# The first pass over the up-projections stores its transposed weight blocks in DRAM, the second pass loads them; late adapter terms, operand slots and the start are reordered

## What is computed

```python
# layer 0: weights quantised to a codebook of 8, plus a rank-64 adapter
lora_delta = lora_B @ lora_A * 0.5
normalized = (weight + lora_delta) / exp(scale_log)          # groups of 128
w_eff = codebook[searchsorted(...)] * scale + lora_delta
x = x + x @ w_eff.T
# layer 1: gated MLP, H = 1024, F = 2752, a rank-16 adapter chosen for each batch row
gate = x @ W_gate.T + 0.5 * (x @ A_gate[i].T) @ B_gate[i].T
up   = x @ W_up.T   + 0.5 * (x @ A_up[i].T) @ B_up[i].T
act  = silu(gate) * up
x = x + act @ W_down.T + 0.5 * (act @ A_down[i].T) @ B_down[i].T
```

## Time and profile before

| | us |
|---|---|
| median of 3 runs | 1616.69 (1616.1 to 1617.36) |
| profiled execution | 1616.32 |
| its span, first to last instruction | 1614.7 |
| PE busy | 1576.9 (98%) |
| DVE busy | 1275.1 (79%) |
| ACT busy | 564.9 (35%) |
| POOL busy | 529.0 (33%) |
| granted TensorE clock, mean | 0.995 |

### The profile page before, as it was taken

How to read it: one execution, slowest core, us unless ns; L and a number is a source line. 1 busy time by engine, 2 the same in 40 slices (tenths; PEclk the granted TensorE clock), 3 DMA queues, 4 the chain that set the end, 5 groups by cost and what they waited for, 6 DMA issues and landing times.

```text
span 1614.7 us, 21155 instructions
## 1 busy us (share of the span) xinstructions
PE 1576.9 (98%) x6968; PEld 1293.7 (80%) x6968; DVE 1275.1 (79%) x1674; ACT 564.9 (35%) x990; POOL 529.0 (33%) x399
## 2 busy tenths in 40 slices
...
GB/s 296 121 112 77 52 200 44 137 168 154 163 149 170 180 178 173 164 289 69 108 103 139 181 178 179 180 180 156 82 205 205 163 182 191 147 227 205 155 189 119
DMA packets 362444, 257.13 MB, mean 159 GB/s; under 512 B 219616, under 2 KB 283360, under 8 KB 362208
## 3 DMA queue, kind: packets, MB, share of 16 engines
...
## 4 chain that ended last, share of the span: by engine, by line
PE 50%; DVE 1%; issue 0%; DVEq 0%
PE bank L1744 10%; PE bank L1967 9%; PE bankC L1967 6%; PE bankA L1744 6%; PE bankC L1744 6%; PE bankA L1967 6%; PE bankT L1967 3%; PE bankT L1785 1%; PE bankT L1786 1%; PE bankC L1760 1%; DVE ql L1417 0%; PE bank L1760 0%; PE bankA L1760 0%; DVE ev L1365 0%; DVE ll L1423 0%; DVE rl L1245 0%
## 5 line engine op out<-in xcount | busy, mean ns | idle before, releaser
L951 ACT CAST rh<-wt 128x512 fp32r<-128x512 f32 x308 | 190.7, 621 | 435.2 <-PE bankC L1760 127.7
L1245 DVE TENSOR_TENSOR rl<-wt,rh 128x512 fp32r<-128x512 f32 x308 | 274.0, 894 | 9.5 <-ACT rh L951 9.1
L1423 DVE TENSOR_TENSOR ll<-ll,lh 128x512 fp32r<-128x512 f32 (+1 forms) x154 | 107.8, 701 | 155.3 <-ACT lh L1060 155.0
L1744 PE MATMUL bank<-xh,rh 128*128 128x512 f32 x528 | 206.2, 391 | 1.1 <-issue 1.1
L1744 PE MATMUL bank<-xl,rh 128*128 128x512 f32 x528 | 205.8, 390 | 0.0
L1744 PE MATMUL bank<-xh,rl 128*128 128x512 f32 x528 | 205.7, 390 | 0.0
L1060 ACT CAST lh<-ll 128x512 fp32r<-128x512 f32 (+1 forms) x154 | 95.6, 621 | 268.6 <-DMA ll<-LT_d 263.5
L817 POOL TENSOR_TENSOR wt<-wt 128x512 f32<-128x512 f32 x44 | 60.1, 1365 | 321.6 <-DVE wt L1239 321.6
L1744 PE MATMUL bankC<-xh,rh 128*128 128x512 f32 x352 | 140.0, 398 | 3.1 <-DVE xl L1254 1.8
L1239 DVE STREAM_TRANSPOSE wt<-wn 128x512 f32<-128x512 f32 x176 | 124.1, 706 | 20.9 <-DMA wn<-Ag_d 9.0
L1744 PE MATMUL bankC<-xl,rh 128*128 128x512 f32 x352 | 139.5, 396 | 0.0
...
## 6 DMA issues: line engine op xcount, KB each, us to landing
ll<-LT_d SPq DMA_DIRECT2D x148, 256.0 KB, 2.9
wn<-in_L_cond_W_gate_dram SPq DMA_DIRECT2D x80, 256.0 KB, 5.2
wn<-in_L_cond_W_up_dram SPq DMA_DIRECT2D x80, 256.0 KB, 5.1
RT_d<-dt SPq DMA_DIRECT2D x70, 256.0 KB, 3.2
ql<-RT_d SPq DMA_DIRECT2D x70, 256.0 KB, 3.8
LT_d<-ev ACTq DMA_DIRECT2D x60, 256.0 KB, 2.5
...
LT_d<-s2a SPq DMA_DIRECT2D x40, 256.0 KB, 4.3
```

The costliest lines, as they stand in the source:

```text
L951: nc.scalar.copy(rh[:, v % RING, 0:KH * rows], wsrc(RSRC[p], rows)).then_inc(s_hi, 1)
L1245: dv.tensor_tensor(rl[:, v % RING, 0:KH * rows], wsrc(RSRC[p], rows), rh[:, v % RING, 0:KH * rows].bitcast(f32), ALU.subtract).then_inc(s_ ...
L1423: dv.tensor_tensor(ll[0:rows, n % NL, :], ll[0:rows, n % NL, :].bitcast(f32), lh[0:rows, n % NL, :].bitcast(f32), ALU.subtract).then_inc(s ...
L1744: last = te.matmul(OUT[p], a[:, u % RING, cols], b[:, OPND[p], k, :], start=k == 0 and n == 0, stop=k == KH - 1 and n == 2 and (p in (0, 1 ...
```

## The change

1. Weights of the second pass. After each transpose of the first pass SP stores the block to `WT_d` (`store_wt`, 256 KB each, 88 in all). In the second pass SP loads the four blocks two blocks ahead (`load_wt`, at p = 5); there is no `load_wn` and no `w_tr` any more. Even blocks lie in `wb`, over the raw-row buffer `wn`, odd ones in `wt`; the sums S1, S2 are shared. POOL's in-place `w_s3` and `w_s4` of the first pass wait for the stores of L21 and L12. The adapter rows of the second pass are loaded to `araw`, transposed once by DVE at (6, 3) into `atr` and written over the stored blocks 0 and 1 by eight small DMAs (`store_wa`, at (7, 1)).
2. Late adapter terms move from counts 6, 7, 8, 9, 13, 14, 15, 16 to 8, 9, 11, 12, 14, 15, 16, 17, with other PSUM banks; `late_lora(h, 0, 0)` now waits for `take` of p = 6 of block m = 0. `store_s`, `a_hi`, `a_lo`, `td` behind them move by one product; the three `silu` of m = 1 move from p = 4 to p = 6, ahead of `ts_hi` there.
3. The adapter matmuls use all 128 partitions; POOL zeroes partitions 96 to 127 of `ts` and `bs` once, at u = 1.
4. First seam: operand slots are reordered, so that the first `x_sum` needs only `LAST0`; the raw x loads go out in another order; `load_wa(0)` on ACT goes from behind `bd_copy(6)` to behind `w_hi(7)`; `hi(3)`, `hi(4)`, `lo(3)`, `lo(4)`, `x_hi(0, 0)` and two `w_tr` of block 1 are moved ahead. The layout of stage C's operands follows the slots.
5. Start: the first `lora_B` load goes from SP to the head of ACT's queue (so four small loads less ahead of the codebook, scale and x loads on SP, and four more ahead of weight and x loads on ACT); DVE does half of its codebook chain before it waits for it; `w_groups(0)` goes ahead of `lora_delta(1)` on PE, and `w_lo(0)` to the head of `quantise(1)`.

```diff
+        LATE_BANK = ((bankC[0:FH, 1, :], bankC[0:FH, 0, :], bankA[0:FH, 1, :], bankA[0:FH, 0, :]),
+                     (bank7[0:FH, :], bank5[0:FH, :], bankC[0:FH, 1, :], bankC[0:FH, 0, :]))
+        LATE_AT = {8: (0, 0), 9: (0, 1), 11: (0, 2), 12: (0, 3), 14: (1, 0), 15: (1, 1), 16: (1, 2), 17: (1, 3)}
-        XORD = R11, T2, R21, T3, T1, T4, R22 = range(7)
+        XORD = R11, T2, R21, T3, T1, T4, R22 = (0, 4, 2, 3, 1, 5, 6)
+        wb = place("wb", [P, 4, KH * P], f32, S0 + 20480)
...
+        def wsrc(mm, n):
+            return wb[:, n, :] if n < 4 and mm >= NH and mm % 2 == 0 else wt[:, n, :]
+        def block_ready(eng, mm, n):
+            if mm < NH:
+                eng.wait_ge(s_tr, 4 * mm + n)
+            else:
+                eng.wait_ge(s_wl[mm % 2], 64 * ((mm - NH) // 2 + 1))
...
+                def store_wt(mm, n):
+                    sp.wait_ge(s_tr, 4 * mm + n + 1)
+                    sp.dma_start(WT_d[mm, n, :, :], wsrc(mm, n)).then_inc(s_wst[n], 16)
+                def load_wt(mm):
+                    if mm == NH:
+                        sp.wait_ge(s_tr, 4 * NH)
+                        sp.wait_ge(s_wal, 16 * 8)
+                    if mm <= NH + 1:
+                        for n in range(4):
+                            sp.wait_ge(s_wst[n], 16 * (mm - 1))
+                    if mm > NH:
+                        sp.wait_ge(s_lo, 7 * (mm - 1))
+                    for n in range(4):
+                        sp.dma_start(wsrc(mm, n), WT_d[mm - NH, n, :, :]).then_inc(s_wl[mm % 2], 16)
...
                 store_x1(LAST0)
-                store_bd(KD - 2)
-                stored(sp, TURN[KD - 2, 1] + 1)
+                stored(sp, KH * NC)
                 load_raw(0, 0, KH, 0, s_x[0])
                 load_raw(1, 0, KH, 3, s_x[3])
+                stored(sp, TURN[KD - 2, 0] + 1)
+                load_raw(0, KH, KD - 1, 2, s_x[2])
+                store_bd(KD - 2)
                 store_x1(LAST1)
+                stored(sp, TURN[KD - 2, 1] + 1)
                 load_raw(1, KH, KD - 1, 6, s_x[6])
-                load_raw(0, KH, KD - 1, 2, s_x[2])
+                for n in range(4):
+                    store_wt(0, n)
+                load_wn(1)
...
+                    if p in (1, 2, 3, 4) and mm + 1 < NH:
+                        store_wt(mm + 1, p - 1)
-                    if p == 3 and 0 <= mm + 2 < NM:
+                    if p == 3 and mm + 2 < NH:
                         load_wn(mm + 2)
+                    if p == 5 and NH <= mm + 2 < NM:
+                        load_wt(mm + 2)
...
                 def w_s3(mm):
+                    if mm < NH:
+                        gp.wait_ge(s_wst[1], 16 * (mm + 1))
...
+                    if u == 1:
+                        stored(gp, NORD)
+                        gp.wait_ge(s_bdst, 16 * KD)
+                        gp.wait_ge(s_sum, 4)
+                        gp.memset(ts[3 * CR:P, :, :, :].bitcast(f32), 0.0).then_inc(s_z, 1)
...
+                        gp.memset(bs[3 * CR:P, :, :, :].bitcast(f32), 0.0).then_inc(s_z, 1)
...
                 hi(1)
                 out_x1(LAST1)
+                x_hi(0, 0)
                 bd_copy(KD - 1)
                 b_hi(0)
                 hi(2)
+                hi(3)
+                hi(4)
                 load_wa(1)
                 out_x1(TURN[KD - 2, 2])
-                x_hi(0, 0)
-                hi(3)
...
                 lo(2)
+                lo(3)
+                lo(4)
                 x_sum(0)
                 x_lo(0, 0)
                 for n in range(1, 4):
                     x_sum(n)
+                w_tr(1, 0)
+                w_tr(1, 1)
                 x_lo(0, 1)
                 x_lo(0, 2)
...
                     for n in range(4):
                         v = u + 7 - n
-                        if v % 7 == 0 and 0 <= v // 7 < NM:
+                        if v % 7 == 0 and 0 <= v // 7 < NH and (v > 7 or n > 1):
                             w_tr(v // 7, n)
...
                 def late_lora(h, m, i):
-                    pe.wait_ge(s_ev, 4 * 2 * NJ * h + 4 * m + (2, 3, 4, 4)[i])
+                    pe.wait_ge(s_ev, 4 * 2 * NJ * h + ((4, 4, 5, 5), (6, 7, 8, 8))[m][i])
...
-                    td_at(u, (4, 6, 8, 10) if first(it - 1) else (0, 4, 7, 10) if it == NJ else (0, 3, 6, 9))
-                    if first(it) and 7 * m + p in (6, 7, 8, 9, 13):
-                        late_lora(h, (7 * m + p - 6) // 7, (7 * m + p - 6) % 7)
-                    if it % NJ == 1 and m == 0 and p < 3:
-                        late_lora(h, 1, p + 1)
+                    td_at(u, (5, 7, 9, 11) if first(it - 1) else (0, 4, 7, 10) if it == NJ else (0, 3, 6, 9))
+                    if u % (14 * NJ) in LATE_AT:
+                        late_lora(h, *LATE_AT[u % (14 * NJ)])
...
+                w_groups(0)
                 lora_delta(1)
-                w_groups(0)
```

More of the change, by code:

```diff
@@ L390, in cond_resid_kernel @@
         s_wa = sem("p1_wa", st)
+        s_wst = [sem(f"p1_wst{i}", st) for i in range(4)]
+        s_wl = [sem(f"p1_wl{i}", st) for i in range(2)]
+        s_wat = sem("p1_wat", st)
+        s_wal = sem("p1_wal", st)
         s_x = [sem(f"p1_x{i}", st) for i in range(7)]
@@ L1059, in l_hi @@
                     act.wait_ge(s_l[n % NL], 16 * (n // NL + 1))
-                    nc.scalar.copy(lh[0:rows, n % NL, :], ll[0:rows, n % NL, :].bitcast(f32)).then_inc(s_lh, 1)
+                    nc.scalar.copy(oph[0:rows, L_AT[n % NL], :], opl[0:rows, L_AT[n % NL], :].bitcast(f32)).then_inc(s_lh, 1)
+                for i in range(NI):
+                    act.dma_start(lb[i * Q:(i + 1) * Q, :, :],
+                                  lora_B[i * DI:i * DI + Q, None, :].to_broadcast([Q, 2, RL])).then_inc(s_lb0, 16)
                 for i in range(NI):
@@ L1134, in _ @@
                 bd_copy(KD - 2)
-                load_wa(0)
                 hi(0)
```

186 lines of the change are left out of this document (109 added, 77 removed).

## The result

The changed kernel takes 1626.01 us (1622.81 to 1628.36, 6 runs), the kernel before in the same comparison 1617.03 (1616.06 to 1618.75): a ratio of 1.0054, with a 95% interval of 1.0041 to 1.0068. It is 0.54% slower; I had forecast 1611.0 and, at the worst, 1617.5. The profiled execution took 1627.25 us, 10.9 more than that of before.

A forecast was written before the change was run, and what follows sets the result against it. PE was taken as the bound, with DVE behind it in two short stretches. 1616.3 - 5.0 (second seam) - 0.3 (first seam) - 0.2 (start) = 1610.8, called 1611.0 against the median; range 1604 to 1617.5.

The forecast's parts named there:

- Second seam, 5.0 won: Start of the second pass, 700 to 800 us: fewer transposes and late adapter terms win 5.0 us, between 2.5 and 8.
- 5 x 0.62 = 3.1 us go: Second seam: five transposes leave DVE's busy stretch, 0.62 us each, so `take` of p = 6 ends 3.1 us earlier.
- rival 3: Second seam's gain goes to new waits, half clock and POOL's sums on `x_lo` (two hits, 2.2 us); 1616, chance 0.22.
- First seam, 0.3 won and at most 3.5 lost: Start of the first pass, 240 to 340 us: 0.3 us won, from 3.5 lost to 3.5 won.
- half clock is as before: First seam: PE's time at half clock stays unchanged, so nothing was added for it.
- It stands later anyway, so I add nothing: First seam: PE may wait 1 to 3 us at product 30 for the copy of product 28, priced at nothing.
- Start, 0.2 won: Kernel start up to the first product, expected at 39.5 to 41.5 us: 0.2 won, between 0.6 won and 1.5 lost.
- The rule of the Trainium skill: Start: queues share the same DMA engines, so the two x loads slow each other; up to 1.4 us later.
- First pass at nothing: First pass, steady: four added stores per block, 1 MB, cost nothing, covered by ACT's and DVE's lead over PE.
- rival 2: First pass: SP and DMA queues become the bound if landing takes about 9 us instead of 5.2; 1622, chance 0.13.
- Over 128 instead of 96 rows: nothing.: Adapter matmuls over 128 instead of 96 rows keep their 512 columns, so they cost or win nothing.
- my signs of being wrong: The second seam keeps its idle time, or the first loses more than 4 us by the store.

The follow-up runs named there:

- f2: Kernel before with 128-row adapter matmuls and the second-pass part alone, block 0's L21 store ahead of raw x loads, store_bs at p = 5; 1614.2 us.
- f3: f1 and f2 together: the kernel after without its new start and first-seam order, with store_bs at p = 5; 1614.12 us.
- f4: f3 with POOL's sums of u = 154 to 161 over 16 of 512 columns, so results differ from the reference; 1605.51 us.
- f1: Kernel before with 128-row adapter matmuls, the late adapter terms, and store_bs at p = 5 in the first block pair; 1615.88 us.
- e3: Kernel after with hi(3), hi(4), lo(3), lo(4) and block 1's two transposes back behind x_sum and the copy of product 28; 1624.23 us.
- g3: Kernel after with SP's two first x loads put behind its scale loads, ACT's queue unchanged; 1619.76 us.
- e2: Kernel after with the next iteration's store_bs for gate at p = 5 instead of p = 3 in each pass's first block pair; 1623.2 us.
- g4: Kernel after with the copy of product 28 on ACT ahead of hi(3) and hi(4); 1627.29 us.
- h2: e2 with the store of L21 of block 0 ahead of the four raw x loads on SP; 1618.07 us.
- h4: h2 with SP's first x loads behind its scale loads, as in g3; 1612.63 us.
- h1: f2 with sums S1 and S2 of blocks 1 and 23 on DVE, the new start, and SP's x loads behind its scale loads; 1610.02 us.
- h3: h1 with the third sum of block 23 also made by DVE instead of POOL; 1611.43 us.
- e4: Kernel before with only the gate and up adapter matmuls over 128 partitions instead of 96, zeros written by POOL at u = 1; 1613.3 us.

## Why the prediction was wrong, point by point

- **Second seam, 5.0 won.** The kernel after won 0.6, the variants with the same code there 1.0 to 3.0, f2 3.3. The failed term is "5 x 0.62 = 3.1 us go". Four of the five transposes lay behind 713.70, 2.5 us; but DVE's stretch from 713.70 (before) and 726.89 (after) to the end of `take` of p = 6 went only from 36.0 to 35.6 us, as POOL's sums of block 23 no longer waited for transposes and fell on `x_lo`, `al` and `lo`. DVE's rows of that stretch, before and then after:

```profile
713.70 2.35 DVE L1254 TENSOR_TENSOR xl<-xr,xh 128x1024 fp32r<-128x1024 f32 x2
719.59 3.93 DVE L1254 TENSOR_TENSOR xl<-xr,xh 128x1024 fp32r<-128x1024 f32 x2
728.96 3.42 DVE L1254 TENSOR_TENSOR xl<-xr,xh 128x1024 fp32r<-128x1024 f32 x2
734.88 3.67 DVE L1254 TENSOR_TENSOR xl<-xr,xh 128x1024 fp32r<-128x1024 f32 x2
```

```profile
726.89 2.35 DVE L1332 TENSOR_TENSOR xl<-xr,xh 128x1024 fp32r<-128x1024 f32 x2
732.16 4.55 DVE L1332 TENSOR_TENSOR xl<-xr,xh 128x1024 fp32r<-128x1024 f32 x2
737.23 3.46 DVE L1332 TENSOR_TENSOR xl<-xr,xh 128x1024 fp32r<-128x1024 f32 x2
743.97 3.43 DVE L1332 TENSOR_TENSOR xl<-xr,xh 128x1024 fp32r<-128x1024 f32 x2
761.28 1.23 DVE L1363 TENSOR_TENSOR ev<-bankC,ev 128x1024 f32<-128x1024 f32 x1
```

  Against 2.35 us for a pair of `x_lo` these are 4.0 us too long before and 4.4 after, and after there come an `al` of 1.75 and a `lo` of 1.76 us, 1.1 each over their 0.68, as in f3: 6.5. These 2.6 us more eat up the four transposes. That is rival 3, and its price of two hits, 2.2 us, was about right; I had left it out of the sum. f4 takes away nearly all such meetings, those of before too: 8.2 us. The 1.1 us that the late terms were to add to the 3.1 are not there either: f1 has +0.4, and f3 wins no more than f2. I had PE's order of waits right: the 5.93 of the earlier trace rows gone, `al` (2.70) and `take` of p = 6 (2.43) in its place, the stall of 0.87 at 787.83 gone (0.9 between u = 170 and u = 175). The half clock that I priced at up to 1.7 a stretch is there twice in the kernel after. The stretch behind `take` of p = 6 makes one product 4.5 us long; e3 and g3 have it too and win 1.0 and 1.6, while in e2, f3, g4, h2 and h4 that product takes 2.9 or 3.0 and they win 2.9 to 3.0.
- **First seam, 0.3 won and at most 3.5 lost.** It lost 10.0. The chain was the predicted one as far as `x_sum(0)`, and so was the issue of L21's store: 219.8 in the time of before, and 223.9 in a kernel that is 4.1 us late by then. The landing is the mis-sized term: I took 6.5 us and it was 8.4, and `w_s3(0)` ran at 232.42. So `x_sum(0)` came 5.2 us later than before against the start, at the bad end that I had worked out (232.4 against 227.11, 5.3), and `take` of p = 6 and u = 8 followed it, 3.3 us late where I had 0.5. h2 shows the remedy: 2.6 us to land if the store goes first, worth 5.1 us. But 6.7 of the 10.0 us come in behind u = 8, where my sum had a gain of 0.8. Of these 3.7 are SP's wait of the next point, for which I had no term; the rest no run takes apart.

  Seen as time of PE, the 10.0 us are 4.2 of half clock and 5.7 of idle time, so "half clock is as before" was wrong too. Between product 20 and u = 25 there were 35 matmuls at half clock instead of 14, and at 0.43 us from start to start instead of 0.23 the 21 more are 4.2 us. PE's idle time is 13.5 us instead of 7.8. The memsets, put at 0.5, cost DVE nothing: while they run, from 252.55 to 255.38, every `x_lo` takes 1.22 us, as ahead of them.
- **What is queued behind a wait, SP.** I moved the late terms on PE and DVE and did not follow `store_bs`, whose wait for them was already 19.1 us long in SP's waits of before. Two to three products later it held `load_wn(3)` and two stores: 3.7 us of the seam and 2.8 of the median (e2).
- **"It stands later anyway, so I add nothing"** (the copy of product 28): right, by g4.
- **Start, 0.2 won.** 3.9 lost. I had the delay of ACT's issue (1.9 us) and took the landing as unchanged. The rule of the Trainium skill stood beside the sum with 1.4 us as its price; g3 shows that it was the main term, 5.3 us at the first tile. The rest of the start wins 0.7 to 3.4 in four kernels (g3, h1, h3, h4), not 0.2.
- **First pass at nothing.** Nearly: the landing of `wn` went from 5.2 to 5.8 and 6.0 us, far from the 9 of rival 2. The table shows 1.3 us of cost against e4 over 125 products (-0.9 and -2.2), in f2 2.7, in part as single waits of PE for `al` and `ad` (0.55 us in the kernel after; 1.00, 0.56 and 0.43 in f2); in the kernel after the longer rows hide it.
- **"Over 128 instead of 96 rows: nothing."** Wrong by 3.4 us, a gain (e4), and the only part of the change that wins by itself.

The start, SP's wait and the second seam have one form: an order was changed, and I priced the instruction that moved or went, not what then ran beside it or was kept waiting. Both of my signs of being wrong came: the second seam kept its idle time, and the place of the store cost the first more than 4 us (5.1 between e2 and h2).
